# Attention pooling over 2048 key sets: second layer half a tile later, a third half-buffer, probabilities issued by another engine, keys in four transfers, another order at the start

## The reference: what is computed

```python
B, L, D, H = (512, 200, 128, 64)      # the inputs have 2048 queries
qe = jnp.broadcast_to(q[:, None, :], k.shape)
feat = jnp.concatenate([qe, k, qe - k, qe * k], axis=-1)
h = feat @ W1 + b1                     # W1: 512 x 64
h = jnp.where(h >= 0, h, alpha[0] * h)
a = (h @ W2 + b2)[..., 0]
a = jnp.where(mask == 0, jnp.float32(NEG), a)
w = jax.nn.softmax(a, axis=-1)
return jnp.einsum('bl,bld->bd', w, k)
```

## Time and profile before

| | us |
|---|---|
| median of three runs | 1019.24 |
| lowest, highest | 1017.79, 1035.44 |
| the profiled execution | 1018.95 |
| its span in the profile | 1017.0 |
| PE busy | 847.9 (83%) |
| DVE busy | 769.4 (76%) |
| POOL busy | 656.3 (65%) |
| PEld busy | 559.4 (55%) |
| ACT busy | 532.8 (52%) |

### The profile page before, as it was taken

The page is one execution under the profiler, slowest core; times in us unless marked ns, Lnnn a source line. Parts: engine busy times, 40 slices in busy tenths (PEclk is TensorE's granted clock), DMA queues, the critical chain, the costliest instruction groups (busy, mean ns, idle before and its releaser), DMA issues.

```text
span 1017.0 us, 55327 instructions
## 1 busy us (share of the span) xinstructions
PE 847.9 (83%) x25216; PEld 559.4 (55%) x25216; DVE 769.4 (76%) x1143; ACT 532.8 (52%) x1281; POOL 656.3 (65%) x401
## 2 busy tenths in 40 slices
PE   0769888988888898889889889888887888888896
PEld 0435555655555565556555556555555555545564
DVE  2879777878788778787787888777886777867771
ACT  0355545655555565555555555555554555545552
POOL 0657666767667676676666667667666667657661
PEclk9899999999999999999998999999999999989999
DMA  8844766667776766786675777766677676667630
GB/s 253 322 148 138 268 204 212 233 201 239 253 236 228 238 206 230 238 270 211 229 231 185 236 266 238 232 223 226 204 242 257 211 230 209 217 225 233 213 103 11
DMA packets 67017, 222.45 MB, mean 219 GB/s; under 512 B 25312, under 2 KB 33504, under 8 KB 66784
## 3 DMA queue, kind: packets, MB, share of 16 engines
q1 hardware_dynamic: 66784, 218.92, 65.0%
HBM read 214.57 MB, written 4.33 MB: 215 GB/s over the span
## 4 chain that ended last, share of the span: by engine, by line
PE 40%; DVE 16%; DMA 15%; issue 13%; ACT 8%; SPq 7%; POOL 0%; DVEq 0%; ACTq 0%; POOLq 0%
PE hP L431 22%; DMA keys<-in_r_k 9%; PE poolP L472 9%; DVE act L348 9%; PE scoreP L460 7%; ACT act L289 6%; DVE keysT L340 5%; DMA probs_scratch<-expd 5%; SPq L160 3%; SPq L211 2%; ACT expd L313 2%; PE poolP L480 1%; DVE neg_max L361 1%; DVE logits L355 1%; DMA w2c<-in_L_rec_W 1%
## 5 line engine op out<-in xcount | busy, mean ns | idle before, releaser
L289 ACT ACTIVATE act<-hP,biast,al 128x200 f32<-128x200 f32 x1024 | 459.5, 515 | 329.6 <-PE hP L431 325.9
L340 DVE STREAM_TRANSPOSE keysT<-keys 128x768 f32<-128x768 f32 (+1 forms) x512 | 510.1, 997 | 60.4 <-DMA keys<-in_r_k 60.3
L431 PE MATMUL hP<-keysT,weff 32*64 32x200 f32 x16384 | 475.5, 344 | 30.3 <-issue 23.5
L232 POOL TENSOR_TENSOR weff<-qX,wp 128x1024 f32<-128x1024 f32 x128 | 244.0, 1906 | 324.3 <-PE hP L431 300.7
L431 PEld LDWEIGHTS hP<-keysT,weff 32*64 32x64 f32 x16384 | 310.2, 133 | 186.2 <-issue 113.1
L348 DVE TENSOR_TENSOR act<-hP,act 128x400 f32<-128x400 f32 x512 | 283.9, 554 | 146.8 <-ACT act L289 143.0
L236 POOL TENSOR_TENSOR weff<-weff,wk 128x1024 f32<-128x1024 f32 x128 | 303.2, 2369 | 10.0
L472 PE MATMUL poolP<-keys,pool_w 128*16 128x128 f32 x6400 | 244.6, 276 | 22.7 <-issue 21.2
L472 PEld LDWEIGHTS poolP<-keys,pool_w 128*16 128x16 f32 x6400 | 173.4, 97 | 98.1 <-issue 93.0
L460 PE MATMUL scoreP<-act,w2win 128*16 128x200 f32 x2048 | 151.3, 341 | 81.3 <-DVE act L348 70.3
L271 POOL TENSOR_TENSOR pool_w<-probs_k,own_b 128x400 f32<-128x400 f32 x128 | 111.3, 870 | 15.7 <-DMA probs_k<-probs_scratch 7.9
(11 more groups left out here) (35 smaller groups left out, 40.9 us busy)
## 6 DMA issues: line engine op xcount, KB each, us to landing
keys<-in_r_k SPq DMA_DIRECT2D x128, 832.0 KB, 5.5
keys<-in_r_k SPq DMA_DIRECT2D x128, 768.0 KB, 5.2
probs_scratch<-expd SPq DMA_DIRECT2D x32, 100.0 KB, 3.7
masks<-in_r_mask SPq DMA_DIRECT2D x128, 12.5 KB
probs_k<-probs_scratch SPq DMA_DIRECT2D x128, 12.5 KB
out_rows<-pooled SPq DMA_DIRECT2D x128, 8.0 KB
keys<-in_r_q SPq DMA_DIRECT2D x4, 256.0 KB, 5.0
act<-in_L_rec_W SPq DMA_DIRECT2D x4, 128.0 KB, 6.1
```

The source lines that it names most:

```text
L232: g_.tensor_tensor(weff[:, n % 2, :, :, :], qX[:, n, :, :].unsqueeze(3).broadcast_to([P, BQ, CD, H]), wp[:].unsqueeze(1).broadcast_to([P, ...
L289: a_.activation(act[:, k, a, :], hP[:, 2 * (p % HSETS) + a % 2, 0:L], ACT.Identity, bias=biast[:, n, k, a:a + 1], scale=al[:]).then_inc(t_ ...
L340: v_.transpose(keysT[:, n % TBUF, j0 * D:j1 * D], keys[:, n % SLOTS, j0 * D:j1 * D]).then_inc(keysT_done, 1)
L431: mm = t_.matmul(hP[H * r:H * r + H, 2 * (p % HSETS) + a % 2, 0:L], weff[QP * a:QP * a + QP, n % 2, w, c, :], kT[QP * a:QP * a + QP, :, c, ...
```

## The change

- Second layer: in step n TensorE does the first half of tile n-1 in the middle and the second half of tile n-1 at the end, each half a tile later than before. `act` has three half-buffers (`ABUF`), used in turn.
- VectorE does the mask and the maximum of a group at the end of a step, behind the activation of pair 4n+2; ScalarE does the exponential and the refill in the step after, between pairs 4n-1 and 4n.
- The write-out of the probabilities and the four reads are issued from ScalarE's list. The write-out stands behind pair 4n, the reads of the first two tiles behind pair 4n+2 of the same step, each behind a wait for the write-out; the other two in the step after.
- Keys go in four transfers (6, 6, 6 and 7 columns), without pacing, once the slot is free. At the start they have no wait for earlier landings either.
- At the start the six parameters are issued first; VectorE transposes the queries ahead of the folding, the first tile's pieces stand between the steps of the bias, and TensorE's wait for the constants moves to where they are used. `neg` is one column, read 200 times over, and `wq` lies in `pool_w`.

The diff, cut to its core:

```diff
+ABUF = 3
-LOADS = 2
-LOAD_CUT = [0, 12, J]
-        act = sb("act", [P, HALVES, QUADS, L])
+        act = sb("act", [P, ABUF, QUADS, L])
...
 # SyncE
-            def load_part(n, x):
-                at = slice(LOAD_CUT[x] * D, LOAD_CUT[x + 1] * D)
-                sp.dma_start(keys[:, n % SLOTS, at], k_tiles[n][:, at]).then_inc(keys_in[n % SLOTS], 16)
+                for x in range(PIECES):
+                    at = slice(CUTS[x] * D, CUTS[x + 1] * D)
+                    sp.dma_start(keys[:, n % SLOTS, at], k_tiles[n][:, at]).then_inc(keys_in[n % SLOTS], 16)
...
             for n in range(1, SLOTS):
-                if n > 2:
-                    sp.wait_ge(keys_in[n - 2], 16 * LOADS)
...
-                        behind = PIECES * (n + 1) + 2 + x * PIECES // LOADS
-                        sp.wait_ge(keysT_done, min(behind, PIECES * TILES))
-                        load_part(n + AHEAD, x)
...
                     sp.wait_ge(part_done, n + AHEAD - SLOTS + 1)
-                paced_part(0)
+                    load_keys(n + AHEAD)
...
-                if n % GT == 0 and 0 <= g < GROUPS:
-                    sp.wait_ge(exp_done, g + 1)
-                    ge(sp, poolw_done, (g - 1) * GT)
-                    sp.dma_start(probs_dram[g % 2], expd[:, g % 2, :]).then_inc(probs_out, 16)
-                    sp.wait_ge(probs_out, (g + 1) * 16)
-                    for t in range(GT):
-                        sp.dma_start(probs_k[:, g % 2, t, :], probs_tiles[g % 2, t]
-                                     ).then_inc(probs_in[GT * (g % 2) + t], 16)
...
 # ScalarE
                 if pair == 0:
-                    ge(act_e, score_done, HALVES * (n - 1) + k + 1)
+                    ge(act_e, score_done, h - ABUF + 1)
...
+            def probs_from(g, t):
+                act_e.wait_ge(probs_out, (g + 1) * 16)
+                act_e.dma_start(probs_k[:, g % 2, t, :], probs_tiles[g % 2, t]
+                                ).then_inc(probs_in[GT * (g % 2) + t], 16)
...
                 scale_pair(PAIRS * n - 1)
-                scale_pair(PAIRS * n)
-                g = n // GT - 1
-                if n % GT == 0 and 0 <= g < GROUPS:
+                g = (n - 1) // GT - 1
+                if n % GT == 1 and 0 <= g < GROUPS:
                     act_e.wait_ge(max_done, g + 1)
...
+                scale_pair(PAIRS * n)
...
+                if moves and n % GT == 1:
+                    ge(act_e, poolw_done, (g - 1) * GT)
+                    act_e.wait_ge(exp_done, g + 1)
+                    act_e.dma_start(probs_dram[g % 2], expd[:, g % 2, :]).then_inc(probs_out, 16)
                 scale_pair(PAIRS * n + 1)
+                if moves and n % GT == 2:
+                    probs_from(g, 2)
                 scale_pair(PAIRS * n + 2)
+                if moves and n % GT == 1:
+                    probs_from(g, 0)
+                    probs_from(g, 1)
+                if moves and n % GT == 2:
+                    probs_from(g, 3)
...
 # VectorE
-                activate(PAIRS * n)
-                if group:
-                    mask_scores(g)
...
                 activate(PAIRS * n + 2)
+                if group:
+                    mask_scores(g)
...
 # TensorE
                 if 0 <= n - 1 < TILES:
-                    second_layer(n - 1, 1)
+                    second_layer(n - 1, 0)
...
-                if n < TILES:
-                    second_layer(n, 0)
+                if 0 <= n - 1 < TILES:
+                    second_layer(n - 1, 1)
```

More of the change, by code:

```diff
@@ L161, in load_mask @@
                                  mask_rows[g, c]).then_inc(mask_in[g % 2], 16)
+            sp.dma_start(al[:], alpha.rearrange("(a b) -> a b", b=1).broadcast_to([P, 1])).then_inc(params_in, 16)
+            sp.dma_start(b2c[:], b2.rearrange("(a b) -> a b", b=1).broadcast_to([P, 1])).then_inc(params_in, 16)
+            for r in range(2):
+                sp.dma_start(b1c[H * r:H * r + H, :], b1.rearrange("(a b) -> a b", b=1)).then_inc(params_in, 16)
+                sp.dma_start(w2c[H * r:H * r + H, :], W2).then_inc(params_in, 16)
             for a in range(QUADS):
@@ L317, in _ @@
                         fill(g + 1)
+                scale_pair(PAIRS * n)
+                if n == 0:
+                    act_e.wait_ge(fold, 11)
+                    fill(0)
                 if m % GT == GT - 1 and 0 <= m < TILES:
@@ L379, in _ @@
             v_.tensor_scalar(wq[:], wq[:], sgn[:], None, ALU.mult).then_inc(fold, 1)
-            dve.wait_ge(q_in, 16 * QUADS)
-            v_.transpose(qX[:].rearrange("p (t y) w c -> p t (w c) y", y=QP), q_sb).then_inc(qx_done, 1)
-            for piece in range(QUADS):
-                transpose_piece(0, piece)
             v_.tensor_scalar(b1s[:], b1c[:], sgn[:], None, ALU.mult).then_inc(fold, 1)
@@ L390, in _ @@
             mm.then_inc(fold, 1)
+            for piece in range(2):
+                transpose_piece(0, piece)
             dve.wait_ge(bias_mm, 1)
@@ L397, in _ @@
             v_.tensor_scalar(biast[:], bias[:], al1[:], None, ALU.mult).then_inc(bias_done, 1)
+            for piece in range(2, 4):
+                transpose_piece(0, piece)
+            dve.wait_ge(shift_mm, 1)
+            v_.tensor_scalar(nshift[:], scoreP[:, 0:GROUPS], b2c[:], -1.0, ALU.add, ALU.mult).then_inc(fold, 1)
             for piece in range(2):
                 transpose_piece(1, piece)
-            dve.wait_ge(shift_mm, 1)
-            v_.tensor_scalar(nshift[:], scoreP[:, 0:GROUPS], b2c[:], -1.0, ALU.add, ALU.mult).then_inc(fold, 1)
             for n in range(STEPS):
@@ L405, in _ @@
                 group = n % GT == 0 and 0 <= g < GROUPS
+                g_late = (n - 1) // GT - 1
+                late = n % GT == 1 and 0 <= g_late < GROUPS
                 transpose_piece(n + 1, 2)
@@ L455, in second_layer @@
                 pe.wait_ge(act_done, PAIRS * n + 2 * k + 2)
+                if n == 0 and k == 0:
+                    pe.wait_ge(fold, 11)
                 if n % GT == 0 and k == 0:
@@ L461, in second_layer @@
                                    w2win[:, HALF_Q - 2 - 2 * t:2 * HALF_Q - 2 - 2 * t],
-                                   act[:, k, a, :], start=(t == 0), stop=(t == HALVES * GT - 1))
+                                   act[:, (HALVES * n + k) % ABUF, a, :], start=(t == 0), stop=(t == HALVES * GT - 1))
                 mm.then_inc(score_done, 1)
@@ L505, in _ @@
             mm.then_inc(shift_mm, 1)
-            pe.wait_ge(fold, 11)
-            pe.wait_ge(consts_done, GT)
             for n in range(STEPS):
```

55 lines of the change are left out of this document (24 added, 31 removed).

## The result

| | us |
|---|---|
| median before, of four runs | 1018.51 |
| median after, of four runs | 1085.79 (1082.70 to 1089.09) |
| ratio | 1.070, 95% interval 1.060 to 1.079 |
| profiled execution after, its span | 1089.09, 1087.4 |

The change makes the kernel 7% slower. The forecast was 984, and 1085.79 lies above the top of its range (1046) and above rival (d) with 1055. Medians take every run; a ratio leaves out runs over 1.5% above the fastest of their kernel.

A forecast was written before the change was run, and what follows sets the result against it. No single engine bounds the kernel; the buffer loop sets the tile at 6.22 us. Group 24.9 + 0.6 + 0.4 + 0.8 + 2.4 = 29.1 against 30.0, -28 us, front -7: 1018.95 to 984 us, range 925 to 1046.

The forecast's parts named there:

- rival (d): Unpaced key queues make code late at every tile and stop the matmuls: group 31.4 us, 1055 us in all; chance 0.17.
- Ordinary tile: Second layer half a tile later, three half-buffers: gains nothing, the buffer loop keeps an undisturbed tile at 6.22 us.
- Rival (b): The tile loop is less rigid; half of VectorE's spare 0.6 us a tile becomes speed: group 27.9, 947 us; chance 0.09.
- Exponential: Moving ScalarE's exponential between two pairs cuts its delay from 1.65 to 0.4 us a group.
- Late keys: Taking the probabilities off SyncE's queue removes VectorE's wait for late keys, 1.6 us a group.
- The 1.25 and the 1.6: Gains in us a group: 1.25 from moving the exponential, 1.6 from keys no longer late.
- Front: At the start, parameters issued first and queries transposed earlier: 7 us saved, first layer at 25 us.
- Keys in four transfers, unpaced: In the main loop, code blocks meeting the long key queue cost TensorE 2.4 us a group, against 1.3 before.
- 24.9 + 0.6: Group of four tiles: 24.9 us for tiles at 6.22, plus 0.6 for the halves with part-adding and whole pooling.
- The 0.8 for the probabilities: Cost a group of late write-out (0.4, ScalarE) and late reads (0.4, GpSimd's weights), in us; bounds 0 to 5.
- rival (c): Probabilities late: GpSimd waits 2 us a group, TensorE for weights; 0.8 becomes 2.4, group 30.7, 1034 us; chance 0.15.
- Rival (a): Waits for code vanish with the hold on the keys: group 26.7 us, 910 us in all; chance 0.10.

The follow-up runs named there:

- keys_back: The kernel after, with keys in the main loop again in the two paced transfers of before: 971.83 us, ratio 0.948.
- both_back: The kernel after, with two paced key transfers and the probabilities' write-out and reads issued by SyncE again: 1022.82 us, ratio 1.003.
- probs_alone: The kernel before, with only the probabilities' write-out and reads issued by ScalarE: 1019.29 us, ratio 0.999.
- half_bytes: The kernel after, with each key transfer from the eleventh tile on cut to 3 columns, 48% of the bytes: 897.46 us, ratio 0.885.

## Why the prediction was wrong, step by step

**Ordinary tile: right.** An undisturbed tile after, TensorE:

```profile
371.53 1.61 PE L433 MATMUL hP<-keysT,weff 32*64 32x200 f32 x64
...
374.19 0.93 PE L433 MATMUL hP<-keysT,weff 32*64 32x200 f32 x32
...
377.76 0.57 PE L433 MATMUL hP<-keysT,weff 32*64 32x200 f32 x12
```

377.76 - 371.53 = 6.23, as before 6.22. 70.3 us of waits at the second layer went and a tile is as long: the loop of buffers was the limit, and the wait has moved to line 433. Rival (b) is out.

**Exponential: right in size, by one tile.** A tile with it, in keys_back, where no code stall disturbs it:

```profile
687.14 1.61 PE L445 MATMUL hP<-keysT,weff 32*64 32x200 f32 x64
...
689.80 0.93 PE L445 MATMUL hP<-keysT,weff 32*64 32x200 f32 x32
691.45 0.94 PE L445 MATMUL hP<-keysT,weff 32*64 32x200 f32 x32 [0.72 <-DVE act L357]
...
693.63 1.61 PE L445 MATMUL hP<-keysT,weff 32*64 32x200 f32 x64
```

6.49, so 0.26 more than 6.23 where 0.4 was taken. Its half is 3.83, not the 3.4 that was to show it, because an undisturbed tile now has halves of 2.66 and 3.57, where it had 3.02 and 3.20.

**Late keys: the wait went** (0.6 us left of 60.3). That this is worth 1.6 a group no run shows. The 1.25 and the 1.6 weren't two separate gains: in both_back the exponential is in its new place and VectorE waits 0.9 us for keys, and nothing is gained, since the probabilities come late there; in probs_alone the late keys are gone, and ScalarE's hold takes the gain.

**Front: right.** -6.0 where -7 was taken. The first layer began at 26.14 where 25 was said, from 33.88:

```profile
26.14 1.25 PE L433 MATMUL hP<-keysT,weff 32*64 32x200 f32 x16 [1.11 <-DVE keysT L337]
```

**The step that failed: "Keys in four transfers, unpaced".** It priced the long queue at 2.4 us a group for code and put at nothing what the same queue does to the probabilities, whose 0.8 was worked out with a landing of 3 us or so. Code itself was under-sized, not wrong in kind: measured 101.7 / 31 = 3.3. The prediction weighed how many of 6.2 blocks would be late, at 0.94 each, and held that the end of each tile's queue would let enough of them through. More were late, 87 / 31 = 2.8 a group (from 55 / 31 = 1.8), and the price was not a constant: 101.7 / 87 = 1.17 on average and up to 3.9. Its base was too small as well: 23.5 us is line 431 alone, and blocks end at lines 472 and 460 too, 54.4 us of code in all or 1.8 a group, where the sum had 1.3 left over. That code alone would give 24.9 + 0.6 + 0.3 + 3.3 = 29.1, the very sum that was forecast, and still faster than 30.0. So the larger part of the miss lies in what the step put at nothing.

**What it put at nothing: the probabilities behind the same queue, and TensorE's own speed.** With 24.9 + 0.6 + 0.3 = 25.8 for the rest:

| kernel | 25.8 + code / 31 | measured | left over |
|---|---|---|---|
| half_bytes | 26.0 | 26.1 | 0.1 |
| keys_back | 27.4 | 28.4 | 1.0 |
| after | 29.1 | 32.4 | 3.3 |

The 0.8 for the probabilities is near the 1.0 of keys_back. In the kernel after 3.3 are left, for the same unpaced keys that make code late make the write-out land at 5.3 instead of 3.2 us. The prediction had this the other way round: against rival (c) it said that both transfers land sooner "at lighter queues".

Rivals (c) and (d) came together. (c) came with its signs, ScalarE held for 57.6 us (1.9 a group), GpSimd waiting 6.2, and TensorE standing for weights, 23.8 us or 0.8 a group. (d) came in part: code cost 3.3, between the forecast's 2.4 and its 4.7. Its sign, over 75 us of "issue" at line 433, is met by the label alone: of those 87.5 us 63.7 are code. They had been given chances as if one excluded the other (0.15 and 0.17), and nothing for both, which by the numbers that stood there, 24.9 + 0.6 + 0.4 + 2.4 + 4.7 = 33.0, give 3.0 more than 30.0, 1018.95 + 93 - 7 = 1105 us.

The other part of the 3.3 is TensorE itself: the same 25216 matmuls were busy for 871.6 us after and 829.3 in keys_back, 1.4 a group, at a mean granted clock of 0.952 against 0.978. In the trace after TensorE works for 96.7 us at the 1.2 GHz level, in keys_back for 38.3. If work there takes twice as long, that is 48.3 and 19.1 us lost, 1.6 and 0.6 a group; this is an estimate from those rows. Together with the late weights (0.8 and 0.5) it is 2.4 of the 3.3, and 1.1 against 1.0 in keys_back. Not all of it need lie on the path: in half_bytes the same two make 0.5 (5.9 and 8.6 us) where 0.1 is left.

Windows of 100 to 880 us, before, after, and half_bytes:

```profile
100.00:880.00 780.00, 676.42 (x20296) 447.09 (x20288) 613.62 (x907) 429.50 (x1036) 528.88 (x312) 0.99 0.70 230
```

```profile
100.00:880.00 780.00, 640.86 (x18679) 440.30 (x18678) 561.92 (x835) 396.26 (x954) 488.10 (x288) 0.96 0.63 210
```

```profile
100.00:880.00 780.00, 724.88 (x23075) 519.67 (x23079) 679.13 (x1021) 491.08 (x1176) 597.67 (x354) 1.00 0.44 128
```

The DMA share is lower after than before, 0.63 against 0.70, and yet more code is late: by these runs the mean load doesn't explain the stalls, and the pacing, by which less is queued at once, does. How the 3.3 divides between clock, ScalarE's hold and late weights wasn't separated by a run; beyond the estimate above it stays open. So does why four transfers, paced, seem a little slower than two.

**Rival (a), and the queue of the probabilities.** Code took 101.7 us in 87 waits; only half_bytes, with 5.0, comes near rival (a). The rule that goes with it, that fetching code is hidden (the Trainium skill, "Runtime: NRT & Kernel Launch", Instruction fetch mechanics), is not what these traces show.

Issued from ScalarE's list, the write-out still landed late behind SyncE's unpaced keys, at 5.3 us; yet with paced keys the move was worth 51 us (keys_back against both_back). By the Trainium skill ("DMA: Bandwidth & Descriptors", Issuing engines are not separate DMA queues) all transfers share the same DMA engines whichever engine issues them, and the first number agrees. The second comes from the place in the list, 6.7 against 3.5 us from the exponential to the first read, which that rule leaves aside.

## What to carry to other kernels

A wait that paces large loads can be worth more than all the slack it seems to waste: look at what else must come through the same DMA engines while the loads are queued, here TensorE's own code every 127 matmuls or so and a small transfer on which another engine's list waits. Before taking such a wait away, count all "issue" idle time of the fast engine over every line, and don't price a late block by today's mean. Place those waits too: here one that falls on the grid of 127 matmuls is code, one that ends 0.10 us behind another engine's row is that engine's. And when two rivals have the same cause, give a chance to both coming at once.

## What was not expected of the hardware

- TensorE's waits for code, which fall on a grid of about 127.2 matmuls, moved with the loads: 5.0 us at 48% of the bytes, 48.5 with two paced transfers, 101.7 unpaced, with the same 198 packets of code each time.
- After such a stall, with TensorE idle for all of 546 to 548 us, the granted clock was 0.85 and then 0.50 in the next two windows of 2 us.
- A 100 KB write issued from ScalarE's list lands at a median of 5.3 us when unpaced keys go out from SyncE's, at 3.2 when they are paced.
